# Expert stage of a sandwich kernel: two matrix products per token replaced by one 128x128 matrix per batch

## What is computed

```python
x = x + layernorm(attention(layernorm(x)))          # 16 heads of 64, masked softmax
u = layernorm(x)
logits = einsum('bh,eh->be', u[:, 0, :], router_w)   # first token of the batch alone
gates  = softmax(top-2 of the 8 logits)              # 8 gates per batch, 6 of them zero
down     = einsum('blh,erh->bler', u, lora_down)     # 128 -> 8 experts x rank 16 = 128
weighted = einsum('bler,ehr,be->blh', down, lora_up, gates)
x = x + layernorm(u + weighted)
```

## Time and profile before

| what | value |
|---|---|
| median of 3 runs | 1085.55 us |
| the runs | 1086.0, 1081.01, 1085.55 us |
| the profiled execution's own time | 1086.26 us |
| its span in the profile | 1084.5 us |
| TensorE's mean granted clock | 0.976 of full |
| busy share of PE, DVE, ACT, POOL | 93%, 54%, 50%, 65% |

### The profile page before, as it was taken

The page is one execution under the profiler, slowest core; times in us unless marked ns, Lnnn a source line. Parts: engine busy times, 40 slices in busy tenths (PEclk is TensorE's granted clock), DMA queues, the critical chain, the costliest instruction groups (busy, mean ns, idle before and its releaser), DMA issues.

```text
span 1084.5 us, 23021 instructions
## 1 busy us (share of the span) xinstructions
PE 1012.8 (93%) x9564; PEld 648.7 (60%) x9564; DVE 588.9 (54%) x995; ACT 539.7 (50%) x736; POOL 703.0 (65%) x503
## 2 busy tenths in 40 slices
PE   3799999999999999999999999999999999999972
PEld 2465666666666666666666666666666665666551
DVE  5545455554556557446546656545555554645454
ACT  4144544554444565554454554555455445454444
POOL 6056666677666767776567778766478676666653
PEclk9599999999999999999999999999999999999996
DMA  3000000001101001001100200010100210100101
GB/s 105 20 2 22 21 3 21 22 22 41 21 21 41 7 17 22 21 21 41 22 2 21 60 21 22 21 22 12 31 22 22 61 21 21 22 2 21 21 21 39
DMA packets 61816, 27.11 MB, mean 25 GB/s; under 512 B 39056, under 2 KB 53776, under 8 KB 61712
## 3 DMA queue, kind: packets, MB, share of 16 engines
q1 hardware_dynamic: 61712, 25.64, 10.1%
HBM read 22.76 MB, written 2.35 MB: 23 GB/s over the span
## 4 chain that ended last, share of the span: by engine, by line
PE 81%; DVE 8%; ACT 8%; issue 2%; POOL 1%; DMA 0%; POOLq 0%; ACTq 0%
PE both L613 23%; PE st L598 15%; PE s_ps L559 8%; PE st L652 5%; PE st L593 5%; DVE least L993 4%; PE st L525 4%; ACT ring L838 3%; PE st L587 3%; ACT total L838 3%; PE both L623 3%; PE st L527 3%; PE st L526 3%; PE s_ps L563 2%; PE st L541 2%
## 5 line engine op out<-in xcount | busy, mean ns | idle before, releaser
L406 POOL TENSOR_TENSOR total<-total,ring 128x1024 f32<-128x1024 f32 (+1 forms) x315 | 543.5, 1725 | 323.5 <-PE both L613 275.8
L993 DVE TENSOR_REDUCE least<-s_ps 128x2 f32<-128x1024 f32 x315 | 312.9, 1010 | 281.4 <-PE s_ps L563 186.9
L838 ACT ACTIVATE ring<-st 128x1024 f32<-128x1024 f32 (+1 forms) x256 | 233.8, 918 | 210.2 <-PE st L598 209.9
L613 PE MATMUL both<-ring,v_sb 128*64 128x512 f32 (+3 forms) x1280 | 210.7, 467 | 0.0
L598 PE MATMUL st<-q_high,k_low 64*128 64x512 f32 (+3 forms) x768 | 173.2, 447 | 0.0
L613 PEld LDWEIGHTS both<-ring,v_sb 128*64 128x64 f32 x1280 | 89.0, 137 | 134.8 <-issue 125.2
L559 PE MATMUL s_ps<-k_high,q_high 64*128 64x512 f32 (+1 forms) x758 | 149.3, 406 | 18.0 <-DVE least L993 13.3
L598 PE MATMUL st<-q_low,k_high 64*128 64x512 f32 (+3 forms) x768 | 132.9, 342 | 0.0
L598 PE MATMUL st<-q_high,k_high 64*128 64x512 f32 (+3 forms) x768 | 132.8, 342 | 0.0
L593 PE MATMUL st<-shift_row,pick 64*128 64x128 bf16 (+3 forms) x1152 | 116.2, 271 | 0.2 <-ACT total L838 0.2
L559 PEld LDWEIGHTS s_ps<-k_high,q_high 64*128 64x128 f32 x758 | 72.4, 188 | 73.2 <-issue 36.3
(11 more groups left out here) (149 smaller groups left out, 1310.5 us busy)
## 6 DMA issues: line engine op xcount, KB each, us to landing
inv_row<-sums_dram SPq DMA_DIRECT2D x62, 256.0 KB, 4.0
x_a<-x SPq DMA_DIRECT2D x4, 512.0 KB, 5.4
sums<-sums_row SPq DMA_DIRECT2D x124, 2.0 KB, 2.1
x_b<-x SPq DMA_DIRECT2D x3, 512.0 KB, 5.7
out<-res_b SPq DMA_DIRECT2D x3, 512.0 KB, 4.3
ring<-w_pairs SPq DMA_DIRECT2D x1, 1152.0 KB, 6.8
shift_row<-shift_t SPq DMA_DIRECT2D x64, 4.0 KB
x_a<-x SPq DMA_DIRECT2D x2, 256.0 KB, 3.1
```

What stands on the lines that cost most here:

```text
L406: nc.gpsimd.tensor_tensor(so_far, so_far, tile_of(n, s)[:, :, col:col + w], ALU.add).then_inc(s_add, 1)
L613: last = nc.tensor.matmul(po[h * D:(h + 1) * D, 0:w], v_sb[(n // 2) % 2][:, j, c0:c0 + D], tile_of(n, s)[:, h, col:col + w], start=(s in F ...
L838: nc.scalar.activation(tile_of(n, s)[:, :, 0:w], st[s % 2][:, :, 0:w], ACT.Exp, scale=SCALE).then_inc(s_exp, 1)
L993: last = nc.vector.tensor_reduce(least[:, :, a:a + 1], bank[:, :, col:col + w], AX.X, ALU.max, negate=True)
```

## The change

It precomputes, for each batch, the matrix that takes `u` straight to its expert output, and applies it in one step:
- `both_ways` is a new 128x128 tensor. At the start it is loaded with what was loaded into `down_sb`; in the fill `c0` PE turns it and DVE copies the turned matrix to `down_sb`. So `down_sb` then holds the down weights with the ranks on the partitions
- the fill `down` becomes `mix`: one product `down_sb` x `up_gated` of 128x128 with 128 columns, which waits for `gate_up`; ACT copies its 128 columns to `both_ways`
- `up` multiplies `u_t` with `both_ways` in place of `up_gated`; `u_t` is not written over any more
- on DVE `make_gate` follows `rank_logits` in the same place (slot 6, g = 0, ahead of taking q and `out`); on ACT `gate_up` moves from the head of slot 6, g = 2 to the end of g = 0, behind the exponentials and the takes
- in the last batch the logits come right behind the turns, then `mix` and its copy, then `up`; both halves of `up` wait for the same things

```diff
         if after and (i, g) == (6, 1):
-            found.append((("down", c - 1, 0), y))
+            found.append((("mix", c - 1, 0), y))
...
-            for dst, src in ((router_sb[:], router_t), (down_sb[:], down_t), (up_sb[:], up_r),
+            for dst, src in ((router_sb[:], router_t), (both_ways[:], down_t), (up_sb[:], up_r),
...
                 elif kind == "c0":
                     need(s_bvw, 1)
                     need(s_small, 16 * 6)
+                    nc.tensor.transpose(dst[:, E:E + P], both_ways[:], ident[:])
...
-                elif kind == "down":
+                elif kind == "mix":
+                    need(s_upg, n + 1)
+                    last = nc.tensor.matmul(dst[:, 0:E], down_sb[:], up_gated[:], start=True, stop=True)
+                elif kind == "up":
                     need_taken("u", n, 0)
+                    need_taken("mix", n, 0)
                     for a in range(2):
-                        half = slice(a * HALF, (a + 1) * HALF)
-                        last = nc.tensor.matmul(dst[:, half], down_sb[:], u_t[:, half], start=True, stop=True)
-                elif kind == "up":
-                    need_taken("down", n, 0)
-                    need(s_upg, n + 1)
-                    for a in range(2):
-                        last = project_up(dg_t, a, dst[:, a * HALF:(a + 1) * HALF])
+                        last = project_up(a, dst[:, a * HALF:(a + 1) * HALF])
...
                 turn_four(y_a, a, st[1][:, a, :]).then_inc(s_last_turn, 1)
+            need(s_first, B)
+            nc.tensor.matmul(s_ps[:, 0, 0:EXPERTS], first_tok[:], router_sb[:], start=True, stop=True).then_inc(s_last_logit, 1)
+            need(s_upg, B)
+            nc.tensor.matmul(both[:, 0, 0:E], down_sb[:], up_gated[:], start=True, stop=True).then_inc(s_last_down, 1)
+            need(s_ut_out, 2)
+            need(s_dg, 1)
             for a in range(2):
-                half = slice(a * HALF, (a + 1) * HALF)
-                need(s_ut_out, a + 1)
-                nc.tensor.matmul(both[:, a, :], down_sb[:], u_t[:, half], start=True, stop=True).then_inc(s_last_down, 1)
-                if a == 0:
-                    need(s_first, B)
-                    nc.tensor.matmul(s_ps[:, 0, 0:EXPERTS], first_tok[:], router_sb[:], start=True, stop=True
-                                     ).then_inc(s_last_logit, 1)
-            need(s_upg, B)
-            for a in range(2):
-                need(s_dg, a + 1)
-                project_up(dg_t, a, st[0][:, a, :]).then_inc(s_last_up, 1)
+                project_up(a, st[0][:, a, :]).then_inc(s_last_up, 1)
...
-                elif kind == "down":
-                    nc.scalar.copy(dg_t[:], src).then_inc(s_free[bank], 1)
+                elif kind == "mix":
+                    nc.scalar.copy(both_ways[:], src[:, 0:E]).then_inc(s_free[bank], 1)
...
-                    if after and (i, g) == (6, 2):
-                        gate_up(c - 1)
                     if 0 <= t < N:
                         for s in T_STEPS[g]:
                             exponentials(t, s)
                     for use, bank in fills(t, g):
                         take(use, bank)
+                    if after and (i, g) == (6, 0):
+                        gate_up(c - 1)
...
-            act.wait_ge(s_first, B)
+            exp_logits(b)
+            gate_up(b)
             act.wait_ge(s_last_down, 1)
-            nc.scalar.copy(dg_t[:, 0:HALF], both[:, 0, :]).then_inc(s_dg, 1)
-            exp_logits(b)
-            act.wait_ge(s_last_down, 2)
-            nc.scalar.copy(dg_t[:, HALF:S], both[:, 1, :]).then_inc(s_dg, 1)
-            gate_up(b)
+            nc.scalar.copy(both_ways[:], both[:, 0, 0:E]).then_inc(s_dg, 1)
...
                 elif kind == "c0":
                     dve.wait_ge(s_small, 16 * 6)
+                    nc.vector.tensor_copy(down_sb[:], src[:, E:E + P])
...
                 elif place == 18:
                     rank_logits(b)
-                elif place == 19:
                     make_gate(b)
```

More of the change, by code:

```diff
@@ L135, in sandwich_kernel @@
         up_gated = sb("up_gated", [P, E])
+        both_ways = sb("both_ways", [P, E])
         minus_half = sb("minus_half", [P, QB])
@@ L173, in sandwich_kernel @@
         u_t = sb("u_t", [P, S])
-        dg_t = u_t
         stats = [sb(f"stats{i}", [P, QB, 6]) for i in range(5)]
@@ L654, in project_out, with project_up @@
                 return last
-            def project_up(src, a, bank):
+            def project_up(a, bank):
                 for j in range(4):
                     t = 4 * a + j
-                    last = nc.tensor.matmul(bank[:, j * P:(j + 1) * P], src[:, t * P:(t + 1) * P], up_gated[:],
+                    last = nc.tensor.matmul(bank[:, j * P:(j + 1) * P], u_t[:, t * P:(t + 1) * P], both_ways[:],
                                             start=True, stop=True)
@@ L860, in take @@
                 kind, n, part = use
-                if kind not in ("q", "k", "v", "m", "sum", "z", "u", "down"):
+                if kind not in ("q", "k", "v", "m", "sum", "z", "u", "mix"):
                     return
```

## The result

The changed kernel takes 1079.62 us in the median (20 runs, 1075.12 to 1084.07), the kernel before 1084.12 (20 runs, 1080.04 to 1086.84). The ratio is 0.9953, with a 95% interval of 0.994 to 0.9967: 5.1 us faster, between 3.6 and 6.5. The prediction had 3.45 us faster and a range of 1078.0 to 1085.3. (Two executions of one experiment's kernel, 1399 and 5099 us, were disturbed and are left out of its numbers.)

A forecast was written before the change was run, and what follows sets the result against it. PE was taken as the bound, with 81% of the chain of waits. Terms -4.5 + 0.15 + 0.0 + 0.9 gave -3.45 us: 1082.8 against the profiled execution, median 1082.1, range 1078 to 1085.3.

The forecast's parts named there:

- What bounds the kernel: Whole kernel and slot 14: PE carries 81% of the chain of waits, and its expert passes are paid in full.
- mix at 0.22, up at nothing: Batches 0 to 2: down's 1.72 us becomes 0.22 (at most 0.65), up unchanged; gain 1.50 a batch, 4.5 us in all.
- The gain is kept; the gate fits before q_low: Slot 6: k_low keeps a margin of 1.1 us; make_gate takes 1.03 between rank_logits and q_low with POOL idle; cost 0.
- Rival (c): Gate meets POOL or k_low's margin shrinks; bank 0 or 1 late by some 1 us per batch: -0.45, 1085.1; chance 0.07.
- c0: Fill c0: one more turn on PE, 0.12 us, and a DVE copy: +0.15 us, bounds 0.1 and 0.5.
- The last batch, first and second term: Last batch: logits read 1.40 us earlier, mix and its copy add 1.4, so up starts where it did; bounds -0.4 to +1.4.
- The third term, the clock: Last batch: up runs at half clock, its first half 2.07 us against 1.19: +0.9, bounds 0 and 1.19.
- Sum: Whole kernel: -4.5 + 0.15 + 0.0 + 0.9 = -3.45 us, 1082.8 against the profiled execution, new median 1082.1.
- The most likely class, the same: Whole kernel: median within about 0.5% (5.4 us) of before, so up to 1080.1 counts as the same; chance 0.77.
- (a): Last batch: tail stays at full clock, up as now, mix a little faster, -0.4; sum -4.75, 1080.8; chance 0.1.
- (b): Slot 6 paced by ACT's exponentials or POOL's adds, PE time saved becomes a wait: +1.05, 1086.6; chance 0.08.
- (d): Batches 0 to 2: mix stands alone on PE, 3 x 0.43 us come back, 1083.3; no chance of its own given.

The follow-up runs named there:

- The experiment with the old place: Changed kernel with make_gate back in front of k_low on DVE and gate_up right before mix's copy on ACT: 1098.99 us, ratio 1.0144 to the kernel before.
- a steady start: 36 unread PE passes ahead of slot 0, added to the kernel before (1079.24 us) and to the changed kernel (1074.33 us), each otherwise untouched.
- change and filler: Changed kernel plus two unread products in the last batch's tail and 36 unread passes at the start: 1073.42 us, ratio 0.9915 to the kernel before.
- the other two with 36 passes: 36 unread start passes added to the changed kernel (1074.33 us) and to its version with the last batch in the old order (1074.11 us); both ratios 0.9925.

## Why the prediction was right, and where it was off

- **What bounds the kernel.** Right. PE is the bound in the slots touched; their length fell by 1.51, 1.51 and 1.50 us, forecast 1.50 each.
- **mix at 0.22, up at nothing.** Right to 0.01 us in slots 14 and 22. In slot 30 `mix` has 0.49 and `down` had 1.98, since no projection of k stands ahead of them there; the difference is 1.5 all the same. The bound of 0.65 was not needed.
- **The gain is kept; the gate fits before q_low.** Right: `k_low` has a margin of 1.2 (forecast 1.1), `make_gate` takes 1.02 (forecast 1.03), POOL idle. The experiment with the old place shows that this step carries all of it. The price beside POOL hangs on when the adds run: the second operation of `make_gate`, with two inputs too, fell between two adds and took 0.17. Rival (c) had a price of 1 us per batch for a late bank; a late gate for `mix` costs 5 to 6.
- **c0.** `c0` has 0.26 + 1.79 us on the chain in place of 1.98: 0.07, forecast 0.15.
- **The last batch, first and second term.** The logits came 1.65 earlier (forecast 1.40) and `mix` with its copy cost 1.22 (forecast 1.4), so that `up` starts 0.43 sooner and not at the same time. The logits' two passes were priced at twice their full-clock time, 0.88; they took 0.63 from load to read (1055.01 to 1055.64). `mix` was priced at 0.98 and took 0.84 from load to copy (1058.80 to 1059.64).
- **The third term, the clock.** In the profile exactly as forecast: half clock, +0.92 (forecast 0.9). As a term of the difference of medians it was sized wrong. The step took the clock of the one profile of before for the rule: in two of four profiles with the old tail `up` runs at half clock too, for all or most of its first half.
- **Sum.** From the profiles, -4.5 + 0.1 - 0.4 + 0.9 = -3.9 against -3.45; with a steady start -4.9. The measured ratio, 3.6 to 6.5 us, holds both; the forecast's 3.45 lies just outside. The median, 1079.62, is 2.5 below the forecast's 1082.1, and 1.4 of that is the kernel before, which over 20 runs has 1084.12 and not 1085.55. It is also below the forecast's own bounds (1080.5): only the allowance for the spread holds it, and that is luck in part. The spread of 5 us was read as noise; it is the clock in the start, and a difference of a few us in a median can come from how many runs fall in which group. The most likely class, the same, holds by the ratio (0.47% against the line of 0.5%), while the median lies below the 1080.1 that was given for it.
- **Rivals.** (a), a tail at full clock, came only with filler. (b), a slot paced by another chain, did not come, nor did (c) or (d) (whose time should read 1083.4).

The Trainium skill, TensorE: Matmul & The Clock Gate, section "The HAM clock gate", says that the monitor runs free of the kernel's start, so that the point of change varies from run to run. The groups of times, the first fall at 24.7 to 27.1 us in six profiles, and the tail at either level agree with that; they don't prove it. The same section puts the penalty of the ramp at a kernel's start below 1% of a typical span and advises against fitting it. The falls here come later, behind waits of PE. They cost 5 to 6 us of 1084 between the outer groups, 0.5%, which is below that 1% and still as much as the whole change.

## What to carry to other kernels

When a matrix depends on the batch and not on the token, multiply the small matrices first, and see to it that what they wait for (here the gate) is made early, at a place where its engine is free and POOL is not adding; a late one costs its wait and can cost the clock behind it. Compare two profiles by their parts (slots, tail), since the clock at the start can differ between executions of one kernel by more than the change is worth. Idle TensorE ahead of dense work can be filled with passes that nobody reads; in the start alone it gave the kernel before a ratio of 0.9964, 3.9 us, not far below the change itself. With change and filler, 1073.42 us and ratio 0.9915 are the lowest, though the intervals of the other two with 36 passes overlap it.

## What was not expected of the hardware

- A wait of PE of 3.62 us in mid-kernel, after dense work, was followed by half clock: `weigh` took 4.86 in place of 3.16 us. A wait can cost half as much again as it lasts.
- A small DVE operation with two inputs, neither from PSUM, that started beside an add of POOL ended 0.02 to 0.03 us behind that add, in all 24 cases of `make_gate`: 0.95 to 1.18 us in place of 0.17. The `TENSOR_SCALAR` of the earlier trace rows did too (414.20, the add 414.17).
- The executions of one kernel form groups, the outer ones 5 to 6 us apart, set by when and for how long the clock falls in the first 60 us: from about 26 us, from about 41 us, or, with 36 passes of filler, not at all (spreads of 0.7 to 2.3 us).
- In slot 30, with PE waiting for ACT several times, the clock fell for 3.4 us in two of the profiles and cost 1.6 us (`up` 3.61 and 3.66 in place of 2.05). The longest wait of PE in the 7 us ahead of the fall was 0.96 us in both, and the same waits stand in the other profiles without a fall.
